# Splitting DVE's long two-operand operations that run beside POOL's gathers and scatters

## The chip, the cores and the metric

The kernel runs on one core of a Trainium2 chip. Its engines are PE (TensorE, matrix multiplies), DVE (VectorE), ACT (ScalarE), POOL (GpSimd, which here mostly issues indirect DMAs) and SP (SyncE, which issues plain DMAs). They share the on-chip memory SBUF (128 partitions); PE writes to PSUM. The metric is the device time of one execution in microseconds (us).

## The reference

A graph of 6250 nodes and 200000 edges, sorted by their target node `dst`; node rows have 128 values. One network with edge weights comes first, then two attention layers, each pair followed by a layer norm:

```python
h = x @ W1 + b1
e = concat([h[dst], h[src] - h[dst]]);  m = relu(relu(e @ W2 + b2) @ W3 + b3)
x = layernorm(x + relu(segment_max(m, dst)))
for layer in range(2):                       # with a self loop for each node
    h = x1 @ C;  e = leaky(h[src] @ att_src + h[dst] @ att_dst)
    alpha = softmax of e over the edges of one dst
    x1 = relu(segment_sum(alpha * h[src], dst) + bias)
out = layernorm(x + x1)
```

## The kernel before

Nodes lie in 49 blocks of 128 (node k*128+p in partition p), and these in 7 batches of 7 blocks (`batches`). Edges lie in columns of 128. Each engine has its own program, written out in order; semaphores join them (`then_inc` counts up, `wait_ge` waits). Nothing reorders the instructions of an engine.

The work runs in these stages:

1. Setup (to some 185 us). POOL gathers rows of dst (L469, `dst_rows` in `ring_a`); DVE counts in them where each node's edges end (`count_rows`, L817 compares, L820 sums). DVE marks where dst changes (L824), scales the marks (L827) and sums them up along each partition (the rank scan, L828). PE projects the nodes (L1260); DVE adds a bias to one half (L846), ACT copies the other (L597), and SP stores that as `Q_table` (L317). POOL waits for this store, gathers the first 16 columns of Q rows (L478), then scatters 49 blocks of P rows (L491). DVE meanwhile prepares `neg` (L881, L884) and splits Q into three bf16 parts with ACT (L907 and L912 on DVE, L606 and L617 on ACT).
2. The node loop (to 2070 us): gather Q rows, place, ReLU, multiply by W3, running maximum.
3. First transition: POOL gathers the last maximum of each node (`gather_ends`, L505), 49 gathers; DVE, batch by batch, makes x (L1023, L1026), its statistics (`spread_of`) and, with PE and ACT, the projection of the batch before (`project`: L1010, L1011 copy attention values, L1014 and L1016 subtract for the bf16 split). POOL then scatters one value of each node (`scatter_ad`, L513), 49 scatters, each batch behind a wait on its `proj_att`.
4. The first attention loop (to 3925 us), 5. the second transition (as the first, with L1201 in place of L1026), 6. the second attention loop (to 5795 us).
7. The tail: 49 gathers, and for each batch DVE's L1196, L1201, L1208, statistics and ACT's normalising; no project.

POOL's indirect DMAs take their list of rows from an SBUF column, `in_offset=...ap=end_i[:, k:k + 1]`. The stages are joined by waits such as these:

```python
pool.wait_ge(proj_att, 6 * (pc + 1))            # scatter_ad: batch pc of the projection is there
vector.wait_ge(node_rows[b], node_value(b, 2))  # DVE: the gathers of batch b have landed
```

## Time and profile before

| | us |
|---|---|
| median of 3 runs | 5897.36 (5895.58 to 5897.44) |
| the profiled execution | 5896.27 |
| its span | 5895.0 |

| stretch, us | PE busy | DVE busy | ACT busy | POOL busy |
|---|---|---|---|---|
| 200 to 2068, node loop | 1622.61 | 908.96 | 585.37 | 1407.06 |
| 2071 to 2207, first transition | 36.84 | 58.92 | 51.76 | 105.08 |
| 2210 to 3925, attention loop | 1596.74 | 1468.97 | 943.34 | 1294.69 |
| 3937 to 4075, second transition | 33.53 | 51.40 | 44.48 | 107.31 |
| 4078 to 5795, attention loop | 1597.74 | 1468.74 | 942.13 | 1296.19 |
| 5807 to 5895, tail | 0.00 | 56.25 | 51.65 | 50.73 |

A timeline row gives the start in us from the span's start, the busy time in us, engine, line, operation, output <- inputs with their shapes, the count (x7 is seven in a row), and in brackets the idle time before it with what ended it. For a row of several, the busy time is that of the whole row. "issue" is time in which an engine waited for nothing that the profile shows.

### The profile page before, as it was taken

The numbers are of one execution on the slowest core, as the hardware profiler recorded it, in microseconds if no ns is written. First come the engines' busy times: TensorE is split into PE (matmuls) and PEld (weight loads), VectorE is DVE, ScalarE is ACT, GpSimd is POOL, SyncE is SP. The second block draws the span as 40 slices with busy tenths as digits, with TensorE's granted clock in tenths as the row PEclk, the third lists the DMA queues.
The fourth block names the chain that finished last, engine by engine and source line by source line (L and its number), as shares of the span: only waits on it lengthen the run. The fifth ranks groups of instructions, "written<-read, shape, count | busy, mean of one in ns | idle before, by whom it ended". The sixth has DMA issues, their size and how long they took to land.

```text
span 5895.0 us, 119772 instructions
## 1 busy us (share of the span) xinstructions
PE 4951.3 (84%) x29442; PEld 3081.7 (52%) x29442; DVE 4092.7 (69%) x10675; ACT 2659.1 (45%) x8225; POOL 4403.0 (75%) x4585
## 2 busy tenths in 40 slices
PE   3588888888888828999999999953999999999991
PEld 2466666666666624555555555532555555555550
DVE  4344444544444448888888888864888888888886
ACT  2233333333333335555555555533555555555554
POOL 6777777777777777777777777767777777777775
PEclk7799999999999959999999999976999999999995
DMA  5687888887777724444444444432444444444443
GB/s 137 179 220 215 216 219 221 217 219 219 216 216 219 206 63 114 123 124 124 124 124 124 124 124 124 125 93 63 124 124 124 124 124 123 124 123 123 124 124 83
DMA packets 808205, 874.81 MB, mean 148 GB/s; under 512 B 133374, under 2 KB 635121, under 8 KB 807754
## 3 DMA queue, kind: packets, MB, share of 16 engines
q0 software_dynamic: 146016, 295.63, 20.9%
q1 hardware_dynamic: 390234, 361.70, 18.8%
q10 hardware_dynamic: 271504, 213.69, 14.0%
q14 instruction: 440, 3.60, 0.2%
q8 instruction: 11, 0.18, 0.0%
HBM read 536.74 MB, written 331.81 MB: 147 GB/s over the span
## 4 chain that ended last, share of the span: by engine, by line
POOL 55%; issue 22%; DVE 7%; PE 6%; DMA 6%; ACT 3%; SPq 0%; DVEq 0%; POOLq 0%; ACTq 0%
POOL ring_a L538 28%; POOL ring_a L478 22%; DMA ring_a<-H_table,src_i 5%; DVE ring_b L1107 4%; PE ps L1404 4%; POOL ring_a L505 3%; ACT ring_a L738 2%; POOL ad_edges L513 2%; POOL P_compact L491 1%; DMA ring_a<-Q_table,src_i 1%; PE ps L1298 1%; PE ps L1308 0%; DVE gz L1091 0%; DVE ring_a L1061 0%; DVE ring_b L1061 0%
## 5 line engine op out<-in xcount | busy, mean ns | idle before, releaser
L538 POOL DMA_INDIRECT ring_a<-H_table,src_i x2712 | 2592.0, 956 | 826.8 <-issue 762.2
L1404 PE MATMUL ps<-work,ring_a 128*128 128x390 bf16 x10752 | 1870.9, 330 | 237.5 <-DVE ring_a L1061 234.8
L478 POOL DMA_INDIRECT ring_a<-Q_table,src_i x1501 | 1434.0, 955 | 476.5 <-issue 461.6
L1404 PEld LDWEIGHTS ps<-work,ring_a 128*128 128x128 bf16 x10752 | 1018.2, 98 | 1065.7 <-DVE ring_a L1061 381.9
L1404 PE MATMUL ps<-work,ring_b 128*128 128x390 bf16 x8064 | 1407.6, 328 | 0.0
L631 ACT ACTIVATE code<-src_row,code_bias 128x128 int16<-128x128 int32 x2676 | 829.6, 389 | 1213.0 <-DVE ring_b L1061 1150.8
L1107 DVE SCALAR_TENSOR_TENSOR ring_b<-ring_b,gw,ring_a 128x129 f32<-128x129 f32 x3124 | 1087.7, 348 | 119.4 <-ACT ring_a L738 103.8
L955 DVE TENSOR_TENSOR_SCAN work<-tab_flat,work,ps 128x512 f32<-128x512 bf16 x390 | 498.1, 1277 | 954.1 <-PE ps L1308 954.0
L1404 PEld LDWEIGHTS ps<-work,ring_b 128*128 128x128 bf16 x8064 | 787.3, 98 | 559.3
L738 ACT ACTIVATE ring_a<-ring_a,gw 128x129 f32<-128x129 f32 x3126 | 959.4, 390 | 0.0
L1061 DVE TENSOR_TENSOR ring_a<-code,ps 128x896 bf16<-128x896 int16 x1536 | 942.1, 613 | 1.6 <-issue 0.3
L641 ACT ACTIVATE work<-ps 128x512 f32<-128x512 f32 x391 | 233.4, 597 | 1093.8 <-PE ps L1298 1062.8
L1061 DVE TENSOR_TENSOR ring_b<-code,ps 128x896 bf16<-128x896 int16 x1152 | 703.8, 611 | 0.0
L1297 PE MATMUL ps<-ident,ring_a 128*128 128x128 f32 x1563 | 448.6, 287 | 255.8 <-issue 168.9
L1298 PE MATMUL ps<-work 128*128 128x128 f32 x3126 | 574.3, 286 | 0.0
L1298 PEld LDWEIGHTS ps<-work 128*128 128x128 f32 x3126 | 506.0, 203 | 4.0 <-issue 0.3
L1308 PE MATMUL ps<-work,W 128*128 128x512 f32 (+1 forms) x782 | 429.0, 632 | 0.0
L1297 PEld LDWEIGHTS ps<-ident,ring_a 128*128 128x128 f32 x1563 | 230.8, 148 | 319.9 <-issue 282.5
L648 ACT ACTIVATE ring_b<-ps 128x512 f32<-128x512 f32 x391 | 232.1, 594 | 269.2 <-PE ps L1318 258.3
L1318 PEld LDWEIGHTS ps<-ident,work 128*128 128x128 f32 x1563 | 204.2, 147 | 226.1 <-issue 225.0
L1088 DVE TENSOR_TENSOR gz<-ring_a,ad_wide 128x8 f32<-128x8 f32 (+2 forms) x394 | 67.5, 171 | 310.8 <-DMA ring_a<-H_table,src_i 301.8
L732 ACT ACTIVATE gw<-gw 128x16 f32<-128x16 f32 (+2 forms) x394 | 84.9, 216 | 388.6 <-DVE gw L1101 387.3
(266 smaller groups left out, 3637.4 us busy)
## 6 DMA issues: line engine op xcount, KB each, us to landing
run_sum<-ring_b SPq DMA_DIRECT2D x388, 520.0 KB
work<-P_compact SPq DMA_DIRECT2D x1563, 64.0 KB
tab_flat<-rank_rows ACTq DMA_DIRECT2D x194, 512.0 KB, 5.4
run_max<-ring_b ACTq DMA_DIRECT2D x194, 512.0 KB
one_rows<-H_table SPq DMA_DIRECT2D x3840, 0.5 KB
ring_a<-H_table,src_i POOLq DMA_INDIRECT x2712
src_row<-in_srcL SPq DMA_DIRECT2D x384, 64.0 KB
ring_a<-Q_table,src_i POOLq DMA_INDIRECT x1501
```

Source lines behind the costliest of these rows:

```text
L478: pool.indirect_dma_start(out=q_ring[:, g % RING, j - j0, :], out_offset=None, in_=Q_table, in_offset=bass.IndirectOffsetOnAxis(ap=srcT_i[ ...
L538: pool.indirect_dma_start(out=h_ring[:, g % RING1, j - j0, :], out_offset=None, in_=H_table, in_offset=bass.IndirectOffsetOnAxis(ap=src_i[ ...
L631: scalar.activation(code[:, c, :], src_row[:, row_slot[at], :], ACT.Identity, bias=code_bias[:, c:c + 1])
L641: scalar.activation(m1T[:, b, 0:n * P], ps[b][:, 0:n * P], ACT.Relu).then_inc(relued, 1)
L738: scalar.activation(h_ring[:, slot, i, 0:F + 1], h_ring[:, slot, i, 0:F + 1], ACT.Copy, scale=gw[:, par, 0, i:i + 1]).then_inc(scaled, 1)
L955: vector.tensor_tensor_scan(scanned[:, b, 0:n * P], b_ring[:, g % RINGB, 1, a * P:(a + n) * P], ps[2 + b][:, 0:n * P], initial, ALU.add, A ...
L1061: vector.tensor_tensor(hot_space[c // 4][:, c % 4, 0:k1 - k0, :], code[:, c:c + 1, :].to_broadcast([P, k1 - k0, P]), blocks_ps[:, 0:k1 - k ...
L1107: vector.scalar_tensor_tensor(out=r_ring[:, slot, i, 0:F + 1], in0=previous, scalar=gw[:, par, 1, i:i + 1], in1=h_ring[:, slot, i, 0:F + 1 ...
L1297: tensor.matmul(piece, lhsT=q_ring[:, g % RING, a + c, :], rhs=ident[:, :], start=True, stop=False, is_transpose=True)
L1298: m = tensor.matmul(piece, lhsT=w_ring[:, g % RING, a + c, :], rhs=onto[:, q % 3, c * P:(c + 1) * P], start=False, stop=True)
L1308: tensor.matmul(ps[2 + b][:, 0:n * P], lhsT=weights["W3"][:, :], rhs=m1T[:, b, 0:n * P], start=True, stop=True).then_inc(multiplied, 1)
L1404: m = tensor.matmul(ps[parity][:, 0:3 * W], lhsT=hot_space[c // 4][:, c % 4, k - k0, :], rhs=split[:, k, :, :].rearrange("p s f -> p (s f) ...
```

## The change

A helper `short` cuts seven blocks of nodes into pieces of three, two and two. DVE's operations on two SBUF operands of one batch are issued piece by piece, and only the last piece counts up the semaphore where others wait on it. The comparison L824 and the one for `neg` (L881) are cut into pieces of 384 columns (the last is shorter), and so is the rank scan: each piece starts from the last value of the piece before and waits for it. Also the sum L820, which has one operand, is cut. Not cut are L778, L780, L837, the single-operand L827 and L884, the scan L1050 and all of the loops. The other engines' programs are the same.

```diff
--- before.py
+++ after.py
@@ -34,6 +34,12 @@
     return groups
+
+
+def short(k0, k1):
+
+    cuts = [k0] + [k for k in range(k0 + 3, k1 - 1, 2)] + [k1]
+    return list(zip(cuts, cuts[1:]))
 
@@ -814,19 +820,27 @@
                 vector.wait_ge(node_rows[b], node_value(b, 1))
-                vector.tensor_tensor(below[:, k0:k1, :], dst_rows[:, k0:k1, :],
-                                     next_n[:, k0:k1].unsqueeze(2).to_broadcast([P, k1 - k0, P]), ALU.is_lt).then_inc(dve.up(), 1)
-                vector.wait_ge(dve.sem, dve.n)
-                vector.tensor_reduce(s["s0"][:, k0:k1], below[:, k0:k1, :], AX_X, ALU.add).then_inc(rows_counted, 1)
+                for a, e in short(k0, k1):
+                    vector.tensor_tensor(below[:, a:e, :], dst_rows[:, a:e, :],
+                                         next_n[:, a:e].unsqueeze(2).to_broadcast([P, e - a, P]), ALU.is_lt).then_inc(dve.up(), 1)
+                for a, e in short(k0, k1):
+                    vector.wait_ge(dve.sem, dve.n)
+                    counted_part = vector.tensor_reduce(s["s0"][:, a:e], below[:, a:e, :], AX_X, ALU.add)
+                counted_part.then_inc(rows_counted, 1)
 
             vector.wait_ge(chunks_loaded, 48)
-            vector.tensor_tensor(fresh[:, 1:BL], chunk_dst[:, 1:BL], chunk_dst[:, 0:BL - 1], ALU.not_equal).then_inc(dve.up(), 1)
+            spans = list(zip(range(0, BL, 3 * P), [*range(3 * P, BL, 3 * P), BL]))
+            for a, e in spans:
+                a = max(a, 1)
+                vector.tensor_tensor(fresh[:, a:e], chunk_dst[:, a:e], chunk_dst[:, a - 1:e - 1], ALU.not_equal).then_inc(dve.up(), 1)
             vector.tensor_tensor(fresh[:, 0:1], chunk_dst[:, 0:1], before[:, :], ALU.not_equal).then_inc(dve.up(), 1)
             vector.tensor_scalar(pair[:, 1, :], fresh[:, :], -BIG, None, ALU.mult).then_inc(pair_made, 1)
-            vector.tensor_tensor_scan(rank[:, :], ones[:, 0:1].to_broadcast([P, BL]), fresh[:, :], 0.0, ALU.mult, ALU.add).then_inc(dve.up(), 1)
-            vector.wait_ge(dve.sem, dve.n)
+            for a, e in spans:
+                vector.tensor_tensor_scan(rank[:, a:e], ones[:, 0:1].to_broadcast([P, e - a]), fresh[:, a:e],
+                                          rank[:, a - 1:a] if a else 0.0, ALU.mult, ALU.add).then_inc(dve.up(), 1)
+                vector.wait_ge(dve.sem, dve.n)
             vector.tensor_copy(total[:, 0:1], rank[:, BL - 1:BL]).then_inc(total_made, 1)
@@ -878,7 +892,9 @@
             vector.wait_ge(dst_loaded, 16)
-            vector.tensor_tensor(neg[:, 1:L], dst_i[:, 1:L], dst_i[:, 0:L - 1], ALU.not_equal).then_inc(dve.up(), 1)
+            for a, e in zip(range(0, L, 3 * P), [*range(3 * P, L, 3 * P), L]):
+                a = max(a, 1)
+                vector.tensor_tensor(neg[:, a:e], dst_i[:, a:e], dst_i[:, a - 1:e - 1], ALU.not_equal).then_inc(dve.up(), 1)
             vector.memset(neg[:, 0:1], -BIG).then_inc(dve.up(), 1)
@@ -904,13 +920,17 @@
                         vector.wait_ge(q_low, n - 1)
-                    vector.tensor_tensor(q_rests[n % 2], q_stage[:, c * PIECE:(c + 1) * PIECE, :], q_split[c][:, :, 0, :],
-                                         ALU.subtract).then_inc(q_rest, 1)
+                    for a, e in short(0, PIECE):
+                        left = vector.tensor_tensor(q_rests[n % 2][:, a:e, :], q_stage[:, c * PIECE + a:c * PIECE + e, :],
+                                                    q_split[c][:, a:e, 0, :], ALU.subtract)
+                    left.then_inc(q_rest, 1)
                 if n >= 1:
                     vector.wait_ge(q_mid, n)
-                    vector.tensor_tensor(q_split[c][:, :, 2, :], q_rests[(n - 1) % 2], q_split[c][:, :, 1, :],
-                                         ALU.subtract).then_inc(q_low, 1)
+                    for a, e in short(0, PIECE):
+                        left = vector.tensor_tensor(q_split[c][:, a:e, 2, :], q_rests[(n - 1) % 2][:, a:e, :], q_split[c][:, a:e, 1, :],
+                                                    ALU.subtract)
+                    left.then_inc(q_low, 1)
 
@@ -1009,11 +1029,15 @@
                     vector.tensor_copy(s["ad"][:, c0:c0 + n], blk[:, :, F + 1]).then_inc(proj_att, 1)
-                at, rest = slice(k0, k1), rest_space[:, 0:(k1 - k0) * W].rearrange("p (k f) -> p k f", f=W)
+                rest = rest_space[:, 0:(k1 - k0) * W].rearrange("p (k f) -> p k f", f=W)
                 vector.wait_ge(split_high, pc + 1)
-                vector.tensor_tensor(rest, tab[:, at, :], split[:, at, 0, :], ALU.subtract).then_inc(split_rest, 1)
+                for a, e in short(k0, k1):
+                    left = vector.tensor_tensor(rest[:, a - k0:e - k0, :], tab[:, a:e, :], split[:, a:e, 0, :], ALU.subtract)
+                left.then_inc(split_rest, 1)
                 vector.wait_ge(split_mid, pc + 1)
-                vector.tensor_tensor(split[:, at, 2, :], rest, split[:, at, 1, :], ALU.subtract).then_inc(split_low, 1)
+                for a, e in short(k0, k1):
+                    left = vector.tensor_tensor(split[:, a:e, 2, :], rest[:, a - k0:e - k0, :], split[:, a:e, 1, :], ALU.subtract)
+                left.then_inc(split_low, 1)
 
@@ -1023,8 +1047,9 @@
                 vector.wait_ge(dve.sem, dve.n)
-                vector.scalar_tensor_tensor(out=x_sb[:, k0:k1, :], in0=E0[:, k0:k1, :], scalar=0.0,
-                                            in1=x_sb[:, k0:k1, :], op0=ALU.max, op1=ALU.add).then_inc(dve.up(), 1)
+                for a, e in short(k0, k1):
+                    vector.scalar_tensor_tensor(out=x_sb[:, a:e, :], in0=E0[:, a:e, :], scalar=0.0,
+                                                in1=x_sb[:, a:e, :], op0=ALU.max, op1=ALU.add).then_inc(dve.up(), 1)
                 vector.wait_ge(dve.sem, dve.n)
@@ -1198,15 +1223,18 @@
                     vector.wait_ge(dve.sem, dve.n)
-                    vector.tensor_tensor(E1[:, at, 0:F], E1[:, at, 0:F],
-                                         bias[name][:, :].unsqueeze(1).to_broadcast([P, n, F]), ALU.add).then_inc(out_summed, 1)
+                    for a, e in short(k0, k1):
+                        left = vector.tensor_tensor(E1[:, a:e, 0:F], E1[:, a:e, 0:F],
+                                                    bias[name][:, :].unsqueeze(1).to_broadcast([P, e - a, F]), ALU.add)
+                    left.then_inc(out_summed, 1)
                     if layer == 0:
                     vector.wait_ge(out_summed, u + 1)
-                    vector.scalar_tensor_tensor(out=x_sb[:, at, :], in0=E1[:, at, 0:F], scalar=0.0,
-                                                in1=x_sb[:, at, :], op0=ALU.max, op1=ALU.add).then_inc(dve.up(), 1)
+                    for a, e in short(k0, k1):
+                        vector.scalar_tensor_tensor(out=x_sb[:, a:e, :], in0=E1[:, a:e, 0:F], scalar=0.0,
+                                                    in1=x_sb[:, a:e, :], op0=ALU.max, op1=ALU.add).then_inc(dve.up(), 1)
                     vector.wait_ge(dve.sem, dve.n)
```

DVE's order in the first transition, from a batch's projection to the next batch's x; `pair` holds the rest for the split, `work` its parts. Before:

```order
L1010 COPY tab_flat<-ps 128x1
L1011 COPY ad<-ps 128x1
L1014 TENSOR_TENSOR pair<-tab_flat,work 128x910
L1016 TENSOR_TENSOR work<-pair,work 128x7x130
L1000 RECIPROCAL rstd<-rstd 128x7
L1002 SCALAR_TENSOR_TENSOR centre<-moments,rstd 128x7
L1023 SCALAR_TENSOR_TENSOR ring_a<-ring_a,negE,b_rows 128x128 x7
L1026 SCALAR_TENSOR_TENSOR x_sb<-ring_a,x_sb 128x896
L990 BN_STATS stats<-x_sb 128x6 x7
```

Now:

```order
L1030 COPY tab_flat<-ps 128x1
L1031 COPY ad<-ps 128x1
L1035 TENSOR_TENSOR pair<-tab_flat,work 128x390
L1035 TENSOR_TENSOR pair<-tab_flat,work 128x260 x2
L1039 TENSOR_TENSOR work<-pair,work 128x3x130
L1039 TENSOR_TENSOR work<-pair,work 128x2x130 x2
L1020 RECIPROCAL rstd<-rstd 128x7
L1022 SCALAR_TENSOR_TENSOR centre<-moments,rstd 128x7
L1047 SCALAR_TENSOR_TENSOR ring_a<-ring_a,negE,b_rows 128x128 x7
L1051 SCALAR_TENSOR_TENSOR x_sb<-ring_a,x_sb 128x384
L1051 SCALAR_TENSOR_TENSOR x_sb<-ring_a,x_sb 128x256 x2
L1010 BN_STATS stats<-x_sb 128x6 x7
```

The two subtractions and the x operation have become three instructions each, in the same places; the seven of one block each between them are as they were.

DVE's order in the setup, from the first count of rows to the ranks; `ring_b` holds the marks, `neg_wide` the ranks, `ad_wide` dst. Before:

```order
L817 TENSOR_TENSOR ring_a<-ring_a,next_n 128x896
L820 TENSOR_REDUCE s<-ring_a 128x7
L824 TENSOR_TENSOR ring_b<-ad_wide 128x1663
L825 TENSOR_TENSOR ring_b<-ad_wide,before 128x1
L827 TENSOR_SCALAR pair<-ring_b 128x1664
L828 SCALAR_TENSOR_TENSOR neg_wide<-ones,ring_b 128x1664
L830 COPY total<-neg_wide 128x1
L832 TENSOR_TENSOR total<-ps,total 128x1
L835 COPY first_rank<-neg_wide 128x13
L837 TENSOR_TENSOR pair<-neg_wide,first_rank 128x1664
```

Now:

```order
L824 TENSOR_TENSOR ring_a<-ring_a,next_n 128x384
L824 TENSOR_TENSOR ring_a<-ring_a,next_n 128x256 x2
L828 TENSOR_REDUCE s<-ring_a 128x3
L828 TENSOR_REDUCE s<-ring_a 128x2 x2
L836 TENSOR_TENSOR ring_b<-ad_wide 128x383
L836 TENSOR_TENSOR ring_b<-ad_wide 128x384 x3
L836 TENSOR_TENSOR ring_b<-ad_wide 128x128
L837 TENSOR_TENSOR ring_b<-ad_wide,before 128x1
L839 TENSOR_SCALAR pair<-ring_b 128x1664
L841 SCALAR_TENSOR_TENSOR neg_wide<-ones,ring_b 128x384
L841 SCALAR_TENSOR_TENSOR neg_wide<-ones,neg_wide,ring_b 128x384 x3
L841 SCALAR_TENSOR_TENSOR neg_wide<-ones,neg_wide,ring_b 128x128
```

The comparison and the scan have become five instructions each, the count of rows three and three; nothing has changed its place.

## Rows read from the trace of the kernel before

**Rows 1.** The page, chain that ended last: shares by engine, then by line.
```profile
POOL 55%; issue 22%; DVE 7%; PE 6%; DMA 6%; ACT 3%; SPq 0%; DVEq 0%; POOLq 0%; ACTq 0%
```

**Rows 2.** Groups by line, POOL, six stretches: count, busy us, mean ns, idle.
```profile
L505 POOL DMA_INDIRECT ring_a<-run_max,end_i x49 | 51.7, 1055 | 25.4 <-issue 14.6 <-DMA run_max<-ring_b 10.7
...
L513 POOL DMA_INDIRECT ad_edges<-ad,start_i x49 | 53.4, 1090 | 14.9 <-issue 14.9
...
L505 POOL DMA_INDIRECT ring_a<-run_sum,end_i x49 | 53.1, 1084 | 16.2 <-issue 14.6 <-DMA run_sum<-fix,fix_i 1.6
...
L513 POOL DMA_INDIRECT ad_edges<-ad,start_i x49 | 54.2, 1106 | 14.9 <-issue 14.9
...
L505 POOL DMA_INDIRECT ring_a<-run_sum,end_i x49 | 50.7, 1035 | 16.2 <-issue 14.6 <-DMA run_sum<-fix,fix_i 1.6
...
L478 POOL DMA_INDIRECT ring_a<-Q_table,src_i x16 | 19.4, 1211 | 12.8 <-issue 12.8
```

**Rows 3.** Timeline, POOL: start us, us, line, operation, idle before.
```profile
93.51 0.94 POOL L478 DMA_INDIRECT ring_a<-Q_table,src_i  x1 [8.28 <-issue]
...
99.77 2.77 POOL L478 DMA_INDIRECT ring_a<-Q_table,src_i  x1 [0.30 <-issue]
...
2082.76 1.03 POOL L505 DMA_INDIRECT ring_a<-run_max,end_i  x1 [0.30 <-issue]
2084.10 1.34 POOL L505 DMA_INDIRECT ring_a<-run_max,end_i  x1 [0.30 <-issue]
...
2113.62 1.69 POOL L505 DMA_INDIRECT ring_a<-run_max,end_i  x1 [0.30 <-issue]
2115.61 1.83 POOL L505 DMA_INDIRECT ring_a<-run_max,end_i  x1 [0.30 <-issue]
...
2197.47 0.98 POOL L513 DMA_INDIRECT ad_edges<-ad,start_i  x1 [0.30 <-issue]
```

**Rows 4.** Timeline, DVE, first transition.
```profile
2081.57 1.93 DVE L1023 SCALAR_TENSOR_TENSOR ring_a<-ring_a,negE,b_rows 128x128 f32<-128x128 f32 x7 [14.02 <-DMA ring_a<-run_max,end_i]
2083.53 1.09 DVE L1026 SCALAR_TENSOR_TENSOR x_sb<-ring_a,x_sb 128x896 f32<-128x896 f32 x1
...
2113.39 1.11 DVE L1014 TENSOR_TENSOR pair<-tab_flat,work 128x910 f32<-128x910 f32 x1 [1.34 <-ACT work L708]
2115.52 1.11 DVE L1016 TENSOR_TENSOR work<-pair,work 128x910 bf16<-128x910 f32 x1 [1.03 <-ACT work L710]
...
2182.47 0.15 DVE L1011 COPY ad<-ps 128x1 f32<-128x1 f32 x1
```

**Rows 5.** Timeline, DVE, setup.
```profile
51.96 0.16 DVE L832 TENSOR_TENSOR total<-ps,total 128x1 f32<-128x1 f32 x1 [5.48 <-PE ps L1251]
...
62.03 1.08 DVE L817 TENSOR_TENSOR ring_a<-ring_a,next_n 128x896 f32<-128x896 int32 x1
...
64.15 1.42 DVE L846 TENSOR_TENSOR tab_flat<-ps,b_rows 128x256 f32<-128x256 f32 x4
66.26 0.42 DVE L846 TENSOR_TENSOR tab_flat<-ps,b_rows 128x256 f32<-128x256 f32 x1 [0.69 <-PE ps L1260]
...
99.61 1.78 DVE L881 TENSOR_TENSOR neg_wide<-dst_i 128x1562 f32<-128x1562 int32 x1
...
101.45 0.97 DVE L884 TENSOR_SCALAR neg_wide<-neg_wide 128x1562 f32<-128x1562 f32 x1
...
105.52 2.08 DVE L907 TENSOR_TENSOR work<-ring_b,ring_a 128x896 f32<-128x896 f32 x2
```

**Rows 6.** DMA issues, 50 to 110 us: KB each, us to landing.
```profile
Q_table<-ring_b SPq DMA_DIRECT2D x1, 3136.0 KB, 11.6
```

**Rows 7.** Timeline, DVE, tail: first operation of two batches.
```profile
5855.39 0.17 DVE L1177 TENSOR_TENSOR two<-ring_a,negE 128x7 f32<-128x7 f32 x1 [0.27 <-DMA ring_a<-run_sum,end_i]
...
5865.05 0.17 DVE L1177 TENSOR_TENSOR two<-ring_a,negE 128x7 f32<-128x7 f32 x1 [0.32 <-DMA ring_a<-run_sum,end_i]
```

## The prediction

> **What bounds the kernel now.** I read the chain that ended last first: 55% of it is POOL, which here issues one indirect DMA after another, and 22% "issue", mostly its pauses between them; DVE has 7% [rows 1]. So a change on DVE counts here by what it does to POOL. Nine tenths of the span are three long loops (the node loop up to 2070 us, two attention loops up to 3925 and 5795 us). The diff touches nothing in them, so they can only start earlier or later. What it touches lies in four short stretches: the setup (to 185 us), the first transition (2071 to 2207 us), the second (3938 to 4075 us) and the tail (5807 us to the end).
>
> So I asked next, for each of these, whether POOL ever waits there and how long its instructions take, in the groups by line of one stretch at a time [rows 2]. In both transitions POOL issues 49 gathers and then 49 scatters, with idle time that is all "issue" (0.30 us each) but for the first wait: nothing there holds POOL but its own instructions. An undisturbed gather takes 0.94 us (at 93.51), a scatter 0.98 (at 2197.47) [rows 3]. The means are higher: 1.055 and 1.090 us in the first transition, 1.084 and 1.106 in the second, 1.035 in the tail. Times 49 that is a loss of 5.4 + 5.4 = 10.8 us, 6.9 + 6.2 = 13.1 us and 4.4 us.
>
> What makes them long is in the two engines' timelines, laid side by side [rows 3, 4]. DVE's subtraction L1014 reads two SBUF tiles from 2113.39 to 2114.50; POOL's gather begins at 2113.62 and ends at 2115.31, 0.81 after it. L1016 runs 2115.52 to 2116.63; the gather begins at 2115.61 and ends at 2117.44, again 0.81 after it, 0.89 late. The gather needs something right at its start that DVE's operation holds until it is over. After such a wait POOL's next start comes 1.1 us after DVE's end, and L1016 starts 1.0 us after L1014's end: one hit sets up the next, which is why the loss is larger than chance would make it.
>
> Does POOL get in between two DVE operations that follow without a pause? L1023 is seven operations on 128 columns [rows 4], back to back in 1.93 us, so a new one every 0.26 us. A gather that begins at 2082.76 [rows 3] in their midst takes 1.03, only 0.09 late; the next begins at 2084.10 inside the 896-column L1026 and is 0.40 late. So POOL waits for the operation in hand, not for the row of them. On this the forecast rests.
>
> **The change part by part.** An 896-column operation (seven nodes) becomes 384 + 256 + 256. Price of the pieces [rows 5]: one of 256 columns (L846) takes 0.42 us, four in a row 1.42, so each further one costs 0.33. Two of 896 (L907) take 2.08; one alone takes 1.09 [rows 4], so they start 0.99 apart. That is 0.66 / 640 = 1.03 ns a column and 0.07 for each start. Three pieces then take 0.46 + 0.33 + 0.42 = 1.21 us where one takes 1.09: 0.12 more of DVE's time for each split. The order of instructions shows no move on POOL, PE, ACT or SP.
>
> The Trainium skill, "VectorE: DVE Perf Modes", section "The DRAIN you can't avoid", says that after every operation the next does not start until the pipe is empty, though one that isn't held starts earlier. By the strict form the pieces would cost 0.56 + 0.42 + 0.42 = 1.40, 0.31 more, and the setup below would pay 3.1 instead of 1.2. The trace has 1.42 for four and not 1.68, so the sum goes by 0.12.
>
> Expected loss on POOL: its starts come every 1.25 us (0.94 + 0.30), so an operation that holds the port for l makes it lose l squared over 2 x 1.25 on average. For 0.46, 0.33, 0.33 that is 0.43 / 2.5 = 0.17 us for a split operation; whole, it is 0.98 / 2.5 = 0.39 by chance, and 0.5 to 0.6 as measured (10.8 and 13.1 over 21 operations each).
>
> *First transition:* seven batches with L1026, L1014 and L1016, 21 operations, all beside POOL. 10.8 becomes 21 x 0.17 = 3.6; saved 7.2. DVE's chain grows by 0.36 a batch. What is late next would be the scatter of the last batch, which needs L1011's copy: that ends at 2182.6 [rows 4], and POOL comes to it at 2197.5 [rows 3]. DVE is 2 us later, POOL 7 earlier, so 5 us of cover are left. *Second transition:* L1201, L1014, L1016, again 21. 13.1 becomes 3.6; saved 9.5. The last scatters hang on the same copy, with no less cover. Bounds of both together: nothing is left of the loss (23.9 saved), or POOL loses a full first block, 0.40, at each of the 42 operations (16.8 left, 7.1 saved). I take 16.7, nearer the free end, by the 0.09 of the gather at 2082.76.
>
> *Tail:* L1201 and L1208 in each of seven batches. Here DVE hardly waits for POOL: a batch lasts 9.66 us (5855.39 to 5865.05), of which 0.27 to 0.32 is idle for a gather's landing [rows 7]. It gains these 0.3 to 0.4 six times, some 2.3 us with the overlap of ends and the longer last one, and pays 0.24 seven times, 1.7. Net 0.6 saved, between 1 us lost (the gathers hold DVE as now) and 1 us saved.
>
> *Setup, what is paid:* five counts of rows (L817, L820) stand among the additions L846 that empty PE's banks. After one, at 62.03, four additions run without a gap, and only the fifth waits for PE again [rows 5]: their banks had been waiting, so PE and the store of Q_table behind them are later by all that the count grows. 2 x 0.12 x 5 = 1.2 us on the store, which needs 11.6 us [rows 6]; POOL's first gather of Q waits for it till 93.51, after 8.28 us of idleness [rows 3]. *What is saved before:* the gathers of dst rows up to 85 us get faster by some 3 us, hidden behind that store; at most 0.7 us, for the traffic of four 64 KB gathers that then doesn't share the store's time (its 3136 KB in 11.6 us). The scan in five blocks is about 0.8 us longer, and DVE sits idle for PE after it anyway, 5.48 us until 51.96 [rows 5]. *What is saved behind:* the 16 gathers from 93.5 us have a mean of 1.211 [rows 2], 16 x 0.27 = 4.3 us lost. The longest, 2.77 at 99.77 [rows 3], outlasts L881 (two shifted views of one SBUF tile) and ends 0.12 behind L884, 0.97 us, a single-operand operation that isn't split [rows 5]. I take 1.0 as left there and 0.1 for each of some ten gathers beside L907 and L912, 1.0 more; saved 2.3 (bounds 0 and 4.3). The setup gives 2.3 - 1.2 = 1.1.
>
> Sum: 7.2 + 9.5 + 0.6 + 1.1 = 18.4 us. The profiled execution took 5896.3 us (span 5895.0), so 5877.9; the median of the three runs is 1.1 above it. Forecast 5879.
>
> **The rivals.**
> *Every block is hit.* A release at a block's end could lock POOL's phase to the next operation, as it does now. For it: the two gathers at 2113.62 and 2115.61, where one hit leads to the next. Against it: the blocks end at three different times, and the longest costs 0.40. Then 7.1 saved in the transitions, nothing net in setup and tail: 5897.4 - 7.1 = 5890.
> *POOL does not get in between blocks.* Between the data of two pieces of 256 or 384 lie 0.07 us; in the row of 128 columns it is 0.26 - 0.13 = 0.13, twice as much. If POOL needs more than 0.07, it waits for the whole group, now 0.12 longer at up to 42 operations: 5.0 more, 1.2 in the setup, and in the tail POOL still holds DVE back and the pieces come on top, 0.24 x 7 = 1.7. 5897.4 + 7.9 = 5905, slower. It decides as soon as most gathers beside L1014 are over 1.5 us. Against it stands that neither gather near L1023 was held for the row, and nothing shows that POOL needs the pause at all.
> *The stretching is not about operands.* The stretches of [rows 3] would have a cause that the split leaves in place (a busy spell of DVE, ACT and DMAs together), and only DVE's extra time stays, 1.2 + 1.7 = 2.9: 5900. The rows speak against it: two subtractions, two gathers, each over 0.81 us behind the subtraction's end. The Trainium skill, "SBUF — State Buffer", section "Who interferes with whom", says that a DVE instruction with two SBUF inputs holds only the shared read interface, against GpSimd's reads, and infers that making DMA descriptors, which needs the write interface, is not held up by tensor_tensor. By that inference the split would free nothing; the trace's two gathers beside tensor_tensor disagree.
>
> **How the numbers follow.** Forecast 0.72; every block hit 0.14; not between blocks 0.09; another cause 0.05. 0.2%, about what a measurement of this kernel tells from no change, is 11.8 us, so faster means below 5885.6. The forecast's own range is 5870 (all losses gone but 2 us) to 5888 (half of them left); nearly all of it is faster. Faster 0.77; same 0.20, from the second case, most of the third and all of the last; slower 0.03, from the third where the loops fall badly. With the second case the range is 5871 to 5891.
>
> **What would show it.** In the new trace POOL's means in the transitions at 1.01 to 1.03 and no gather over 1.4 there but beside the unsplit scan L1050; L1014's three pieces at about 0.56, 0.42, 0.42, 0.33 to 0.46 apart; the first gather of Q near 94.5 us; the first transition 7 us shorter, the second 9 to 10, the loops unchanged within 2 us. It is wrong if POOL's long gathers stay at 1.7 to 1.9, if they only move to other operations (L1023, L1196), or if a loop takes back what it gets.

## The result, and the profile after

The change took the kernel from 5897.18 us (median of 7 runs, 5892.13 to 5897.82) to 5874.62 us (7 runs, 5871.82 to 5877.45): 22.6 us less, ratio 0.9964, 95% interval 0.9954 to 0.9973. The forecast was 5879.0 with a range of 5871 to 5891. The profiled execution has a span of 5872.3 us against 5895.0, so the two traces differ by 22.7 us, the medians by 22.6.

POOL's share of the chain that ended last falls [rows 1]:

```profile
POOL 49%; issue 21%; DVE 10%; PE 9%; DMA 7%; ACT 4%; SPq 0%; DVEq 0%; POOLq 0%; ACTq 0%
```

The groups by line for POOL, in the same six stretches as [rows 2] (first transition's gathers and scatters, second's, tail's gathers, Q's gathers in the setup), with count, busy us, mean ns and idle time. In the new file L505 is L511, L513 is L519 and L478 is L484:

```profile
L511 POOL DMA_INDIRECT ring_a<-run_max,end_i x49 | 48.3, 986 | 25.8 <-issue 14.6 <-DMA run_max<-ring_b 11.2
...
L519 POOL DMA_INDIRECT ad_edges<-ad,start_i x49 | 49.8, 1016 | 14.9 <-issue 14.9
...
L511 POOL DMA_INDIRECT ring_a<-run_sum,end_i x49 | 47.4, 967 | 16.3 <-issue 14.6 <-DMA run_sum<-fix,fix_i 1.6
...
L519 POOL DMA_INDIRECT ad_edges<-ad,start_i x49 | 49.4, 1008 | 14.9 <-issue 14.6 <-DVE ad L1031 0.3
...
L511 POOL DMA_INDIRECT ring_a<-run_sum,end_i x49 | 46.9, 958 | 16.2 <-issue 14.6 <-DMA run_sum<-fix,fix_i 1.6
...
L484 POOL DMA_INDIRECT ring_a<-Q_table,src_i x16 | 16.2, 1011 | 15.1 <-issue 15.1
```

The means went from 1055, 1090, 1084, 1106, 1035 and 1211 ns to these. The column of idle time is the second thing to see: but for the first wait of each group of gathers it still is "issue", so POOL was not handed a new wait. (0.3 us in the second transition is one usual pause that now ends with the copy L1031, formerly L1011: the cover that the prediction had spoken of is used up there, and no more.)

One hit, close up. POOL's timeline in the first transition, and DVE's beside it, to be held against [rows 3, 4]:

```profile
2113.50 1.20 POOL L511 DMA_INDIRECT ring_a<-run_max,end_i  x1 [0.30 <-issue]
2115.01 0.94 POOL L511 DMA_INDIRECT ring_a<-run_max,end_i  x1 [0.31 <-issue]
2116.25 1.12 POOL L511 DMA_INDIRECT ring_a<-run_max,end_i  x1 [0.30 <-issue]
2117.68 1.15 POOL L511 DMA_INDIRECT ring_a<-run_max,end_i  x1 [0.30 <-issue]
```
```profile
2113.32 1.24 DVE L1039 TENSOR_TENSOR work<-pair,work 128x390 bf16<-128x390 f32 x3 [1.03 <-ACT work L716]
...
2115.16 1.92 DVE L1047 SCALAR_TENSOR_TENSOR ring_a<-ring_a,negE,b_rows 128x128 f32<-128x128 f32 x7
2117.11 1.23 DVE L1051 SCALAR_TENSOR_TENSOR x_sb<-ring_a,x_sb 128x384 f32<-128x384 f32 x3
```

The gather at 2113.50 begins 0.18 us into L1039, inside its first piece. Whole, that operation made such a gather last 1.7 to 1.8 us; now it is 1.20, and it ends 0.81 us after the first piece (which is over at 2113.89), as the gathers of [rows 3] ended 0.81 after the whole operation: the 0.26 lost is the rest of one piece. The next one begins after the operation and is undisturbed.

Where the 22.7 us are, counted between the starts of the same POOL instructions in both traces (POOL's order is unchanged, so its first gather or scatter of each stretch is a fixed mark):

| stretch | before | after | difference | forecast |
|---|---|---|---|---|
| start to first gather of Q | 93.51 | 92.35 | -1.16 | +1.2 |
| to the first scatter of P | 24.25 | 21.05 | -3.20 | -2.3 |
| to the first transition (node loop) | 1953.78 | 1955.46 | +1.68 | 0 |
| first transition | 136.53 | 129.52 | -7.01 | -7.2 |
| attention loop, layer 0 | 1729.91 | 1728.22 | -1.69 | 0 |
| second transition | 138.26 | 127.72 | -10.54 | -9.5 |
| attention loop, layer 1 | 1731.38 | 1730.39 | -0.99 | 0 |
| tail, to the end | 87.40 | 87.56 | +0.16 | -0.6 |

### The profile page after: what moved, and what is told of

Read it like the earlier page. It is cut to its first block, busy times and chain, and to the rows that moved or that the text cites. A ratio compares the mean times of both kernels' runs of the same rounds, so it can differ in the third digit from the quotient of the medians.

```text
span 5872.3 us, 119952 instructions
## 1 busy us (share of the span) xinstructions
PE 4938.4 (84%) x29442; PEld 3069.0 (52%) x29442; DVE 4108.1 (70%) x10855; ACT 2658.9 (45%) x8225; POOL 4372.4 (74%) x4585
## 4 chain that ended last, share of the span: by engine, by line
POOL 49%; issue 21%; DVE 10%; PE 9%; DMA 7%; ACT 4%; SPq 0%; DVEq 0%; POOLq 0%; ACTq 0%
POOL ring_a L544 25%; POOL ring_a L484 20%; DMA ring_a<-H_table,src_i 5%; PE ps L1432 5%; DVE ring_b L1132 5%; ACT ring_a L744 2%; POOL ad_edges L519 1%; POOL ring_a L511 1%; DMA ring_a<-Q_table,src_i 1%; PE ps L1326 1%; POOL P_compact L497 1%; PE ps L1336 1%; PE ps L1325 1%; DVE ring_a L1086 1%; DVE gz L1116 0%
## 5 line engine op out<-in xcount | busy, mean ns | idle before, releaser
L484 POOL DMA_INDIRECT ring_a<-Q_table,src_i x1501 | 1431.0, 953 | 479.6 <-issue 463.2
```

What stands on the lines that cost most here:

```text
L484: pool.indirect_dma_start(out=q_ring[:, g % RING, j - j0, :], out_offset=None, in_=Q_table, in_offset=bass.IndirectOffsetOnAxis(ap=srcT_i[ ...
```

## The experiments

The experiments ran on three other chips, and each of these ran the kernel before in 7777 to 7789 us, not in 5897. On them a difference of 20 us is hard to tell from the spread between runs (7745 to 7845 for the kernel before), so the experiments are read mainly from their traces. What POOL loses beside DVE can be read there as well as here: "loss" below is the sum of what each gather takes over 0.945 us and each scatter over 0.98. Most files have the lines of the changed kernel at 5 more (L1035, L1039 and L1051 are L1040, L1044 and L1056); the PSUM kernel has the lines of before, and experiment 7 those of the changed kernel.

**What those chips do.** The kernel with PSUM operands, layer 0's attention loop:

```profile
4006.37 0.33 PE L1404 MATMUL ps<-work,ring_b 128*128 128x390 bf16 x1 [1.16 <-issue]
...
4008.46 0.33 PE L1404 MATMUL ps<-work,ring_b 128*128 128x390 bf16 x1 [1.76 <-issue]
...
4405.73 8.31 SPq L376 DMA_DIRECT2D one_rows<-H_table  x12
```

PE has all it needs (its idle time says "issue", no releaser) and still starts a product only every 2 us for a while. SP needs 8.31 us for twelve issues that take 4.83 us in the trace of before (at 4401.90). POOL's gathers are not slower, 0.95 and 0.30 between. It looks as if PE and SP got their instructions late at times on these chips; no run shows that, nor why.

**1. The transitions alone.** Setup and tail as before: `short(k0, k1)` back to one piece everywhere but in L1035, L1039, L1051 and L1227 of layer 0.

```
-                for a, e in short(k0, k1):        (count_rows, marks, Q's pieces, scan, tail)
+                for a, e in whole(k0, k1):
```

> Only the operations of the two transitions are split (the projection's two subtractions, the first layer norm's x, the bias sum of the first attention layer); setup and tail are whole as before. Theory (POOL waits for the DVE operation in hand, and in the transitions nothing else holds POOL): first transition 7 us shorter, from the first E0 gather to the first gather of the attention loop, second 10 to 11 us shorter, the rest within 2 us of before; 5879 to 5881 in all. Rival (most of the gain came from the setup or from loops that fell well): no more than 10 us faster than before, above 5886.

Measured: 7786.47 us, ratio 1.0009 (0.9987 to 1.0031). Once more on another chip:

> Only the edits of the two transitions (pieces of L1014, L1016, L1026 and L1199 in layer 0) are in; setup and tail are as before. The same kernel as the first of these runs, whose chip ran the kernel before in 7777 us, where loops set more than the gathers did; this asks for the time on a chip that runs the kernel before near 5897. My theory: the two transitions shrink by what POOL's scatters and gathers lose there, 7.0 and 10.5 us in the trace of the changed kernel, and the loops by another 0 to 2: 17.5 to 19.5 us faster, 5878 to 5880, ratio 0.9967 to 0.9970. Rival (the transitions' gain is given back in the loops, whose first slice starts with fewer gathers ahead): under 10 us faster. Rival (setup and code placement have the gain): about 5895.

Measured: 7781.69 us, ratio 0.9994 (0.9973 to 1.0015). Neither chip was one that could tell the two accounts apart by time. By the traces: loss in the gathers of the first transition 1.2 us in both, against 2.4 to 2.7 in the four traces with whole operations (experiments 2 and 3); in the scatters 0.7 and 1.0 against 6.9 to 7.3; in the scatters of the second transition 0.8 and 0.8 against 8.9 to 9.0. This edit frees POOL by itself. The transitions don't get shorter for it as expected, though. The first takes 163.8 and 163.6 us (whole 162.1 to 163.3), where 7 less was expected, and the second 153.1 and 153.2 (whole 153.7 to 153.9), where 10 less was. The scatters' stretch in layer 0 is even longer, 101.4 and 101.2 us, whole 98.1 to 99.6. Experiment 6 shows why.

**2. The setup alone.** `short` and the scan's blocks in the setup only.

```
-                for a, e in short(k0, k1):        (transitions, tail)
+                for a, e in whole(k0, k1):
```

> Only the setup's operations are split, transitions and tail whole. Theory as predicted (2.3 us saved on the Q gathers, 1.2 paid by the counts of rows): the P scatters end 1 us earlier than before, 5896. Theory with PE's clock: in the trace of before PE's granted clock is at half between 56 and 59 us, beside the first projections, and in that of the changed kernel it is not; where it stays up, the Q table's store starts 0.8 us earlier instead of 1.0 later and the P scatters end 4 us earlier, 5893; where it falls, they end 2 to 2.5 us earlier, 5895. Transitions as long as before, within 1 us, in either case.

Measured: 7793.65 us, ratio 1.0015 (0.9992 to 1.0039). Again:

> Only the setup's edits are in (count_rows, rank, marks, the scan by 384, Q's pieces). My theory: the first Q_table gather starts 1.1 to 1.5 us later than the kernel before would by its additions, but the gathers from there to the first P_compact scatter lose 1.1 instead of 4.3 us; a net 2 to 3 us faster, 5894 to 5895. If the 1.2 us by which the changed kernel's first gather was earlier is the edit's own and not PE's clock in that one execution, 4.4 us faster, 5893. Rival (count_rows' pieces are on the path in full and POOL's losses come back in the first rounds of the node loop): within 1 us of the kernel before. First gather after Q_table's store: 93.5 in the trace of before, 92.4 in that of the changed kernel; here 92 if it is the edit's own, near 94.5 if it is not.

Measured: 7808.55 us, ratio 1.0022 (1.0007 to 1.0037): slower here, which neither account had. Two things happen. From the first gather of Q to the first scatter of P it is 21.3 us in both traces, in those with a whole setup 23.1 to 23.6, loss 1.3 against 3.1 to 3.6: that saving is the edit's. But the first gather of Q is 111.2 and 112.6 us behind the first in_dst gather, against 95.5 to 99.8 us in the eight traces with a whole setup. PE's timeline, first the setup whole (experiment 1, first run), then cut (experiment 2, second run):

```profile
39.63 14.57 PE L1281 MATMUL ps<-work,W 128*128 128x512 f32 x26 [2.95 <-issue]
```
```profile
42.33 1.86 PE L1281 MATMUL ps<-work,W 128*128 128x512 f32 x2 [0.19 <-issue]
...
47.15 2.00 PE L1281 MATMUL ps<-work,W 128*128 128x512 f32 x2 [2.96 <-ACT work L602]
51.35 2.08 PE L1281 MATMUL ps<-work,W 128*128 128x512 f32 x2 [2.20 <-issue]
```

The same 26 products run in one row, or in pairs some 4.2 us apart (3 to 5 in the other traces), each pair waiting for ACT and ACT for it. The granted clock is the other half of it. Windows of the changed kernel (experiment 7), then of a kernel with the setup whole (experiment 8); the columns are the busy time of PE, PE's weight loads, DVE, ACT and POOL, then PE's granted clock and the DMA's share and GB/s:

```profile
41.00:49.00 8.00, 5.82 (x6) 1.67 (x6) 6.71 (x11) 0.76 (x2) 6.48 (x6) 0.50 0.29 96
49.00:57.00 8.00, 6.29 (x7) 1.57 (x7) 0.00 (x0) 2.75 (x4) 5.88 (x7) 0.50 0.15 49
```
```profile
41.00:49.00 8.00, 7.82 (x12) 2.40 (x10) 4.78 (x4) 3.43 (x5) 7.00 (x4) 0.65 0.20 68
49.00:57.00 8.00, 6.37 (x17) 2.31 (x16) 1.52 (x3) 5.07 (x9) 5.96 (x7) 1.00 0.16 49
```

With the setup whole PE is busy for 7.82 of 8 us and its clock rises to the upper level (2.4 GHz); with it cut PE has gaps and stays at the lower one (1.2 GHz), while ACT and PE wait for each other. All four traces with a cut setup have it: the 26 products take 42 to 49 us at a mean clock of 0.50 to 0.58. None of the eight others has: 14 to 15.5 us at 0.79 to 0.89. More than half of that comes back behind them, since the projection L1293 then takes 25 us instead of 42 to 46. On the chip of the result the changed kernel ran the 26 in one row too, 14.34 us, at a mean clock of 0.81. What about the cut goes with the gaps on the slower chips is open. DVE is not in that chain, and a single gap is not enough: three of the traces with a whole setup have one of 0.9 to 1.0 us early in the row and recover. The place of the instructions in the programs may matter; that was not tried by itself.

**3. The tail alone.**

```
-                for a, e in short(k0, k1):        (setup, transitions)
+                for a, e in whole(k0, k1):
```

> Only the tail is split (the bias sum and the x of the second attention layer), all else whole. Theory (the tail's gathers get 3 to 4 us faster, but DVE and ACT are then the ones behind, and the pieces cost what the gathers free): the last gather 3.8 us earlier after the first of the tail, the end within 0.5 us of before, 5897. Rival (the tail follows POOL): 3 to 4 us faster, 5893 to 5894.

Measured: 7792.78 us, ratio 1.0023 (0.9999 to 1.0048). Again:

> Only the tail's edits are in (L1199 and L1189 in the last layer in pieces). My theory: the last gather starts 3.8 us earlier and the end does not move, since seven batches of DVE work at 9.5 us stand behind it: 0.2 us slower to 0.3 faster, 5897. Rival (what is late in the tail is the landing of the gathers): 2 to 4 us faster, 5893 to 5895.

Measured: 7799.05 us, ratio 1.0009 (0.9992 to 1.0026). The gathers take 60.8 and 60.3 us (whole 61.9 to 62.6), but from the last one to the end it is 62.0 and 65.2 us, against 54.3 to 55.8 in the nine traces with a whole tail that ran on these chips. There the tail's cut costs 5 to 8 us net; on the chip of the result it cost 0.2. That it gives nothing is shown; its price depends on the chip. In the changed kernel's trace DVE no longer waits for a gather's landing behind the first one (the 0.27 to 0.32 of [rows 7] are gone, 2.0 us in all), but a little longer for ACT, 7.2 us in the tail instead of 6.2:

```profile
5833.73 0.17 DVE L1211 TENSOR_TENSOR s<-ring_a,two 128x7 f32<-128x7 f32 x1 [0.49 <-ACT two L758]
...
5835.09 2.06 DVE L1221 SCALAR_TENSOR_TENSOR ring_a<-ring_a,two,tab_flat 128x128 f32<-128x128 f32 x7 [0.55 <-ACT tab_flat L761]
```

**4. Is it the operands?** The kernel before, uncut, but L1014 and L1016 take their second operand from PSUM. It leaves out the split of the table into three bf16 parts and is read for its timing only.

```
-    vector.tensor_tensor(rest, tab[:, at, :], split[:, at, 0, :], ALU.subtract)
+    vector.tensor_tensor(rest, tab[:, at, :], ps[5][:, 0:W].unsqueeze(1).to_broadcast(...), ALU.subtract)
```

> The kernel before, nothing split; but the projection's two subtractions (910 columns) take their second operand from PSUM (a bank's first 130 columns, repeated), so that they read one SBUF tile each. The split of the tables into bf16 parts is therefore not computed. Theory (what holds POOL is the second SBUF operand, not DVE's being busy): these operations are as long as before, within 0.1 us, and no gather or scatter beside them is over 1.1 us; what stays in the transitions is the loss beside the x operation and the bias sum, 0.3 to 0.5 each; the first transition 6 to 8 us shorter. Rival (any long DVE operation holds POOL, or DVE's writes do): gathers of 1.7 to 1.8 us beside them as before, the transition no shorter than by 1 us.

Measured: one run, 7771.09 us. DVE's and POOL's timelines, first of this kernel, then of experiment 3 (second operand in SBUF):

```profile
2563.69 1.10 DVE L1014 TENSOR_TENSOR pair<-tab_flat,ps 128x910 f32<-128x910 f32 x1 [1.34 <-ACT work L708]
...
2563.13 0.98 POOL L513 DMA_INDIRECT ad_edges<-ad,start_i  x1 [4.55 <-DVE ad L1011]
2564.42 0.98 POOL L513 DMA_INDIRECT ad_edges<-ad,start_i  x1 [0.30 <-issue]
2565.71 0.98 POOL L513 DMA_INDIRECT ad_edges<-ad,start_i  x1 [0.30 <-issue]
```
```profile
2562.43 1.11 DVE L1040 TENSOR_TENSOR pair<-tab_flat,work 128x910 f32<-128x910 f32 x1 [1.34 <-ACT work L719]
2564.56 1.11 DVE L1044 TENSOR_TENSOR work<-pair,work 128x910 bf16<-128x910 f32 x1 [1.03 <-ACT work L721]
...
2561.86 0.98 POOL L524 DMA_INDIRECT ad_edges<-ad,start_i  x1 [4.32 <-DVE ad L1036]
2563.15 1.24 POOL L524 DMA_INDIRECT ad_edges<-ad,start_i  x1 [0.30 <-issue]
2564.70 1.83 POOL L524 DMA_INDIRECT ad_edges<-ad,start_i  x1 [0.30 <-issue]
```

The second scatter of each begins at the same place, 0.72 us into an operation of the same length: 1.24 us with both operands in SBUF, 0.98 with one in PSUM. Eleven scatters of the one trace begin at that place (1.24 to 1.26 us) and twelve of the other (0.98 to 0.99). The third scatter doesn't compare, since in the PSUM kernel it begins just before L1016; but a gather of the first transition begins 0.17 us into it and takes 0.94 us, where in the traces with whole operations one that begins 0.09 to 0.16 us in takes 1.80 to 1.84:

```profile
2474.78 1.10 DVE L1016 TENSOR_TENSOR work<-pair,ps 128x910 bf16<-128x910 f32 x1 [1.03 <-ACT work L710]
2474.95 0.94 POOL L505 DMA_INDIRECT ring_a<-run_max,end_i  x1 [0.30 <-issue]
```

Over layer 0's 49 scatters the loss beside these two operations is 6.7 us in one kernel and none in the other; what is left in the PSUM kernel, 3.5 us, stands beside the uncut L1026, which still has two SBUF operands. The rival that put the stretching down to something else falls with this, and so does one that blames DVE's writing, which is the same in both. The size was missed: the first transition is 161.4 us long against 163.2 in the two traces with whole operations from the same chip, 1.8 shorter and not 6 to 8.

Two more things stand in the traces. The hold depends on who comes first. A gather that begins 0.00 to 0.03 us into such an operation is not held; DVE's operation is then 0.05 us longer. One that begins 0.06 us in or later is held to its end, but for its last 0.1 us or so. From the setup of before:

```profile
109.83 1.08 DVE L912 TENSOR_TENSOR ring_a<-work,ring_a 128x896 bf16<-128x896 f32 x1
109.98 1.75 POOL L478 DMA_INDIRECT ring_a<-Q_table,src_i  x1 [0.30 <-issue]
...
112.02 1.13 DVE L912 TENSOR_TENSOR work<-work 128x896 bf16<-128x896 f32 x1
112.03 0.94 POOL L478 DMA_INDIRECT ring_a<-Q_table,src_i  x1 [0.30 <-issue]
```

And two SBUF operands are not the only case. Each of the eleven gathers in these traces that begin 0.07 us or more inside a one-operand TENSOR_SCALAR or COPY over 1562 or 1563 columns of SBUF (L1047, L884 and L1052 of before and their likes) also ends 0.81 to 0.82 us behind that operation's end: one that begins 0.24 us into L1047, at 2213.12 in the trace of before, takes 1.55. No experiment changed one of these.

**5. Two pieces** of four and three blocks in the transitions, all else whole.

```
-    cuts = [k0] + [k for k in range(k0 + 3, k1 - 1, 2)] + [k1]
+    cuts = [k0, k0 + 4, k1]
```

> Only the two transitions are cut, into two pieces of four and three blocks instead of three pieces. On the two chips met so far, which run the kernel before in 7780 us, times can't tell 10 us; so this is read by POOL's loss in the transitions (its gathers above 0.945 and scatters above 0.98 us). My theory: a descriptor-making instruction is held from where it meets an operation on two SBUF operands to that operation's end, so the loss goes with the piece's length: a piece of four blocks is 0.62 to 0.64 us long against 0.42 and 0.56, and one instruction meets at most 0.35 of it. Loss behind the first scatter of layer 0: 6.9 with the operations whole, 0.6 to 0.8 with three pieces; with two 1.3 to 2.5. Rival (all that matters is that there is a joint at all): as with three pieces, 0.6 to 0.8. On a chip that runs the kernel before near 5897: 13 to 17 us faster.

Measured: 7779.59 us, ratio 0.9989 (0.9967 to 1.0011). The loss in layer 0's scatters is 6.1 us, near the 6.9 to 7.3 of whole operations, not the 1.3 to 2.5 I had worked out; in the gathers it is 0.9, no worse than with three pieces. One batch of scatters, two pieces:

```profile
2523.85 1.18 DVE L1040 TENSOR_TENSOR pair<-tab_flat,work 128x520 f32<-128x520 f32 x2 [1.34 <-ACT work L719]
2526.06 1.17 DVE L1044 TENSOR_TENSOR work<-pair,work 128x520 bf16<-128x520 f32 x2 [1.03 <-ACT work L721]
...
2523.29 0.98 POOL L524 DMA_INDIRECT ad_edges<-ad,start_i  x1 [4.48 <-DVE ad L1036]
2524.57 1.31 POOL L524 DMA_INDIRECT ad_edges<-ad,start_i  x1 [0.30 <-issue]
2526.19 1.42 POOL L524 DMA_INDIRECT ad_edges<-ad,start_i  x1 [0.30 <-issue]
```

On these chips the first scatter of each batch waits for DVE's copy L1036. From then on both engines run by fixed delays, and all batches look alike: the second scatter (2524.57) begins just after the start of the second piece (2523.85 + 0.62 = 2524.47), the third just after the start of L1044. With three pieces the second scatter begins near the end of a piece and lasts 1.04. A chance formula, which I had used, counts hits as if POOL came at any moment; where both engines start from one event, the same hit is met in each batch that starts so (six of the seven here) or never. For the gathers, which don't wait for DVE, it did no better in this comparison: it has two pieces lose more than three, and they lost 0.9 us against 1.2.

**6. Seven pieces** of one block.

```
-    cuts = [k0] + [k for k in range(k0 + 3, k1 - 1, 2)] + [k1]
+    cuts = list(range(k0, k1 + 1))
```

> Only the two transitions are cut, into seven pieces of one block. My theory: a piece is some 0.25 us long, of which it costs DVE 0.06; no POOL instruction is held by more than 0.15, the loss behind the first scatter of layer 0 goes from 0.7 (three pieces) to 0.1 to 0.5, and each operation takes DVE some 1.5 instead of 1.21 us, which shows in the scatters' stretch of a chip whose instructions come slowly (101 us with three pieces, 99.5 with whole ones) as 103 or more. Rival (more joints, more holds: each piece that starts under a descriptor-making instruction holds it anew): a loss above 1.5. On a chip that runs the kernel before near 5897: within 2 us of the three pieces.

Measured: 7811.20 us, ratio 1.0021 (1.0001 to 1.0042). Loss in layer 0's scatters 0.8 us, as with three pieces (0.7 and 1.0), so nothing more is to be had; but DVE pays.

```profile
2533.83 1.55 DVE L1040 TENSOR_TENSOR pair<-tab_flat,work 128x130 f32<-128x130 f32 x7 [1.45 <-ACT work L719]
```

1.55 us where three pieces take 1.24 and one 1.11, which is 0.07 us for each piece more, as [rows 5] had it. The scatters' stretch is 108.9 us long against 101.2. On these chips that stretch is DVE's: POOL waits 45.4 us there for L1036, with three pieces 37.4 to 37.9, with whole operations 28.1 to 29.9. It is the answer to experiment 1: what POOL no longer loses, it waits for.

**7. The change again.**

> The changed kernel itself once more, unchanged. If the chip runs the kernel before near 7780: the setup's cut cost 15 us there (first Q_table gather 111 to 113 us behind the first of in_dst's, 95.5 to 98 with the setup whole), the tail's and the transitions' nothing that shows: my theory is 10 to 20 us slower, ratio 1.0013 to 1.0026, whose first cause is the 100 instructions more of the setup. Rival (the setup's 15 us are those two kernels' placement of code and not the cut): ratio 1.000 and a first gather at 96. If the chip runs it near 5897: 0.9955 to 0.9975.

Measured: 7818.51 us, ratio 1.0037 (1.0014 to 1.0061): slower by 29 us (11 to 47) where the same file was 22.6 us faster on the chip of the result. Against the traces with the same stretch whole, its setup is 14 us longer, its tail 7, the scatters 2 and 1; Q's gathers (2.3) and the transitions' gathers (1.5 each) are shorter. That makes some 19 us; the rest is not located, since the loops differ by tens of us from trace to trace.

**8. The attention scan too.** The longest gather of the new trace, 4.21 us at 2204.85, stands beside the uncut scan L1075 (1563 columns). It is cut by 384 columns; first with the setup cut but for the sum of `count_rows`, and the tail whole:

```
-                vector.tensor_tensor_scan(ring_b[:, L:2 * L], keep, ad_exp[:, :], 0.0, ...)
+                for a, e in zip(range(0, L, 3 * P), [*range(3 * P, L, 3 * P), L]):
+                    vector.tensor_tensor_scan(ring_b[:, L + a:L + e], keep[:, a:e], ad_exp[:, a:e],
+                                              ring_b[:, L + a - 1:L + a] if a else 0.0, ...)
+                    vector.wait_ge(dve.sem, dve.n)
```

> The changed kernel with three edits of its own: the attention scan L1050 of the rank rows (one operation over 2048 columns on two SBUF operands, beside which one gather or scatter took 4.21 us after and 3.5 in layer 1) is cut by 384 columns as the other scan is; the tail and the reduction behind count_rows (L820) are whole again. My theory: a gather that meets the scan gets in between its pieces, so POOL loses about 0.5 instead of 3.2 us, once in each layer; the five joints cost DVE 0.1 to 0.4 each, off the path; the tail gives 0.2 back, the reduction 0.2 to 0.5. In all 3 to 6 us under the changed kernel: 5869 to 5872, ratio 0.9953 to 0.9958. Rival (the joint of two scans is no gap, since each waits for the one ahead and its result comes on at once, so the gather is held through): 5874.5. Rival (a scan's start value read from SBUF costs each piece a microsecond and puts DVE on the path): 5878.

Measured: 7798.98 us, ratio 1.0021 (1.0004 to 1.0038), with the setup's 15 us in it. Then with setup and tail whole:

> The transitions in three pieces and the attention scan L1050 by 384, setup and tail as before. My theory: POOL's gathers beside the scan lose 1.9 instead of 3.3 us in each layer, so this is the fastest of the kernels with the setup whole: on a chip near 5897, 20 us faster than before (5877); on one near 7780, where loops are not the gathers', within 10 us of the kernel before, with the setup's first gather at 96 us. Rival (the scan's five pieces take DVE 1.0 us more on the path to the first attention round): no faster than the transitions alone.

Measured: 7789.35 us, ratio 0.9996 (0.9975 to 1.0017), where the transitions alone had 1.0009 and 0.9994: no gain that could be told. The trace of the first of the two, POOL beside the scan:

```profile
2612.71 1.32 POOL L549 DMA_INDIRECT ring_a<-H_table,src_i  x1 [0.30 <-issue]
...
2612.94 0.97 DVE L1077 TENSOR_SCALAR ring_b<-neg_wide 128x1563 f32<-128x1563 f32 x1
...
2614.01 4.43 DVE L1081 TENSOR_TENSOR_SCAN ring_b<-ring_b,ad_wide 128x384 f32<-128x384 f32 x5
...
2614.34 1.38 POOL L549 DMA_INDIRECT ring_a<-H_table,src_i  x1 [0.31 <-issue]
2616.03 0.94 POOL L549 DMA_INDIRECT ring_a<-H_table,src_i  x1 [0.30 <-issue]
2617.27 1.61 POOL L549 DMA_INDIRECT ring_a<-H_table,src_i  x1 [0.30 <-issue]
2618.47 1.21 DVE L1084 COPY ad_wide<-ring_b 128x1563 f32<-128x1563 f32 x1
2619.18 1.31 POOL L549 DMA_INDIRECT ring_a<-H_table,src_i  x1 [0.30 <-issue]
```

POOL gets in between the scan's pieces, so the rival of a held row falls for scans too. But the five gathers still lose 0.38 + 0.44 + 0.67 + 0.37 = 1.9 us, where 0.5 was expected and the two of the changed kernel's trace lose 0.18 + 3.27 = 3.4, and DVE takes 4.43 us instead of 3.42. At best 1.6 us a layer. Two of the four losses aren't the scan's: the gather at 2612.71 is over before it begins and stands beside the TENSOR_SCALAR L1077, and the one at 2619.18 ends 0.81 us behind the COPY L1084, both one-operand operations. The copy behind the scan has a share in the 4.21 us, too: that gather ends 1.12 us behind the scan, 0.31 later than the usual 0.81.

No experiment ran on a chip like the one of the result. Which of these versions is best there is open; by its trace it would be the change with the tail left whole, by an estimated 0.2 us that no time could tell.

## Why the prediction was right, and where it was off

*The mechanism.* "POOL waits for the operation in hand, not for the row of them": right, and shown from both sides, by the pieces (no gather of the transitions above 1.29 us and no scatter above 1.33 any more) and by the PSUM operand. The trace had already spoken against the inference that the prediction cites from the Trainium skill, "SBUF — State Buffer", section "Who interferes with whom", that tensor_tensor would not hold up the making of descriptors; experiment 4 now does so with a single operand changed, for indirect DMAs. These also read their list of rows from SBUF, and no run tells whether it is that reading or the making of descriptors that waits.

*The transitions.* 7.2 and 9.5 forecast, 7.0 and 10.5 measured; POOL's losses went from 10.8 to 3.7 and from 13.0 to 2.4 us, where 3.6 each was worked out. That this was so near is partly luck, as experiment 5 shows: 0.17 us for each split operation assumes that POOL comes at any moment. In the second transition it came at better moments, in the first at about average ones.

*The price of a piece.* 1.21 us for three was forecast, 1.24 with 390 columns and 1.23 with 384 measured: right. By the strict form of the Trainium skill, "VectorE: DVE Perf Modes", "The DRAIN you can't avoid", it would have been 1.40 by the prediction's estimate.

*The setup* is where the forecast was off, by 3.3 us, by two terms. First, the additions behind a count of rows: the count's extra time is there (from one count to the next 5.70 us instead of 5.43, four times, 1.0 in all), but the first gather of Q is 1.2 us earlier, not 1.0 later. I had taken PE's part of that stretch as given. Windows of before, then of after:

```profile
54.00:56.00 2.00, 1.45 (x6) 1.29 (x7) 1.97 (x4) 0.00 (x0) 1.69 (x2) 0.89 0.45 162
56.00:58.00 2.00, 2.00 (x7) 1.53 (x6) 1.27 (x3) 0.50 (x2) 1.39 (x3) 0.50 0.95 331
```
```profile
54.00:56.00 2.00, 1.57 (x7) 1.44 (x8) 1.97 (x7) 0.00 (x0) 1.70 (x2) 1.00 0.41 155
56.00:58.00 2.00, 2.00 (x11) 1.75 (x10) 1.72 (x5) 0.90 (x3) 1.39 (x3) 1.00 0.93 318
```

Before, the granted clock fell to the lower level for about 3 us, after PE had stood from 51.9 to 54.6; after, PE stood for as long (51.8 to 54.4) and it did not fall, and the additions from the third on come 1.8 us earlier. The store's 0.4 us (11.2 instead of 11.6 to landing) makes up the rest: 1.0 - 1.8 - 0.4 = -1.2. (The prediction had allowed at most 0.7 there; four gathers of 64 KB at the rate of its 3136 KB in 11.6 us would be 0.9. It used neither in the sum.) Whether that clock is the edit's gift is open. On the other chips the cut setup is the one with the lower level in the 26 products, but the higher one (0.89 to 0.91 against 0.70 to 0.76) in this stretch behind them. So 1.8 of the 22.7 us can't be credited to the mechanism. Second, the losses behind the first gather of Q: 2.3 was taken between bounds of 0 and 4.3, and 3.2 came. I had left 1.0 us beside the uncut L884. The gather that met the pieces of L881 no longer runs into it; the next one begins 0.49 us into it (now L900) and takes 1.30 us, the longest left, 0.36 lost. In the trace of before the 2.77 us gather ends 1.15 us behind L881, 0.34 later than the usual 0.81, so L884 had no more than that share in it.

*The tail.* 0.6 saved was forecast, within 1 us either way; it was 0.2 lost. The gathers finish 3.8 us earlier and buy nothing, since DVE passes on to the next wait, ACT's. The term of 2.3 us for landings was near: 2.0 us of such waits are gone. But DVE's waits for ACT grew by 1.0 us, which the sum had at nothing, and the 14 operations pay 0.14 each instead of 0.12, 2.0 in all where 1.7 was taken. That would be 1.0 lost; why it was only 0.2 isn't traced.

*The loops* moved by +1.7, -1.7 and -1.0 us, within the 2 us of the forecast, and nothing in them was to be attributed.

*The sum.* 18.4 forecast, 22.7 measured: setup 3.3 more, second transition 1.0 more, loops 1.0, against 0.2 in the first transition and 0.8 in the tail.

## What to carry to other kernels

Where POOL sets the pace and makes descriptors, look at what DVE does at the start of each POOL instruction that is longer than its kin: an operation on two SBUF operands holds it to its end, and pieces of a third to half a microsecond free it for 0.07 us each. A one-operand copy or TENSOR_SCALAR over 1563 columns of SBUF holds it too in these traces, and this change left those whole. Cut only where POOL is the one that is waited for; where DVE is on the path (this tail, or these scatters on other chips) the same cut costs, and moving one operand to PSUM, if it can live there, frees POOL at no price in the operation's own time (1.10 us against 1.11). And where both engines start from one event, don't average over chance: lay the two timelines side by side for one batch.

## What was not expected of the hardware

The same file took 5874.6 us on one chip and 7818.5 on another, with PE idle without a releaser and SP's issues 0.69 us apart instead of 0.40; a ratio of 0.9964 there was 1.0037 here. A cut in DVE's work alone went with PE's clock staying at the lower level in 26 products of the setup of those chips, 14 us net. And one POOL gather can be held by 3.27 us (4.21 beside the 3.42 us scan and the copy behind it), so the hold has no limit below that.
